# Reordered first products, a third gate bank, four column groups and eight products on a cleared region

## The chip, the cores and the metric

The kernel runs on one core of one Trainium2 chip. The time is the device time of one execution in microseconds (us), from the first to the last instruction and a little around them. The kernel before was timed in three runs; the traces come from one further execution, taken by the hardware profiler.

## The reference, cut to what matters

64 query tokens of 512 features attend to 6272 context rows of 512 features, and two more stages follow on the same 64 tokens. All of it is 32-bit.

```python
q  = layernorm(x) @ Wq + bq                 # 64 tokens, 32 heads of 128
k, v = split(ctx @ Wkv + bkv)               # 6272 keys, 8 key/value heads of 128
x  = x + softmax(q k^T / sqrt(128)) v @ Wo + bo      # 4 query heads share one key head
# quantised 4-bit weights W = NF4[codes] * scales, each with a rank-16 term (A, B)
z  = layernorm(x)
a  = (lin(z, Wq') + lin(z, Wk') + lin(z, Wv')) / 3
x1 = z + lin(a, Wo')
h  = silu(lin(x1, Wg)) * lin(x1, Wu)        # 1792 wide
x  = x + x1 + lin(h, Wd)                    # Wd: 1792 -> 512, low rank: (h A_down^T) B_down^T
x  = x + base and Fourier products of layernorm(x)
```

## The kernel before, in words

**The long loop.** The keys lie in 7 chunks of 896 (`CHUNK`), and each chunk is worked through for 8 key/value heads: 56 blocks. In a block TensorE (queue `pe`) makes the keys of the next head (`project_keys`), the scores of this head (`scores`), for every second head the values (`values`), it turns the probabilities (`turn_probs`) and multiplies those of the head before by the values (`prev_values`). Each 32-bit operand is split into a high part, rounded by ScalarE (queue `act`), and a low part, which VectorE (queue `dve`) makes by subtraction; a product is then three products (`split_matmuls`, L73 to L75). Beside that GpSimd (`pool`), ScalarE and VectorE expand one tile of the quantised weights per block: GpSimd narrows the codes (`narrow`) and makes four of eight straight lines (`line`), ScalarE four (`lines`), VectorE takes their maxima (`merge`), GpSimd joins and scales them (`join`), and the SyncE queue (`sp`) stores the tile in DRAM (`tile_out`). 56 tiles go out so; the last two, `NB` and `NB+1`, are kept in SBUF as `extra`.

**The order.** Each engine runs one list of instructions in the order written, held by semaphores. There is no planner: where a step stands in the list of its queue sets when it can run.

**The start.** `sp` loads x, the identity `ident` (both count on the semaphore `x_in`), chunks of the context, the query weights head by head (`load_wq`) and the key/value weights in eight pieces (`load_wkv`); `act` loads piece 0 and two parts of the context. VectorE normalises x once both x and `ident` are there (L1465), TensorE turns it (L875), VectorE copies it (L1477). Then the first keys are made: ScalarE rounds piece 0 and the four parts of the first context chunk (`round_wkv`, `round_first`), VectorE makes the low parts (`split_wkv`, `split_first`), and TensorE does 24 products, six for each part k (L880 to L882). After them come the query of head 0 (`query_product`, `query_turn`), then on ScalarE the keys' high parts (`round_keys`), the query's copy (`query_out`) and piece 1, on VectorE the keys' low parts (`split_keys`), the query's bias and split (`finish_query`) and piece 1. Only then the first block begins with its scores. GpSimd clears the first half of `acc`, the running output, right at the start (L576, semaphore `cleared`).

**The end.** After the last block TensorE projects the attention out and works through the quantised stage with weight tiles from a ring of 22 slots of two tiles each, which `sp` fills in order (`load_slot`); the loads from slot 35 on stand behind `scales_of(NB + 1)`, which waits until GpSimd has scaled tile `NB`. The gate and up products are made in three pairs of 256 columns each and a last half (`gated_pair`, `gated_last`), in two PSUM banks in turn (`GU_BANKS`); ScalarE takes the exponent, VectorE makes silu times up (L1552 to L1570, `h_ready`), TensorE turns the result (`turn_gated`, `h_turned`), VectorE copies it (`gated_t`, `h_t`), and six slots of the down weights follow (slots 40 to 45), then 14 small products for the low rank (`low_down`), the two tiles of `extra` and the low-rank product with `lb_d`. `late` are the loads of `lb_d` and the bias `bb_sb`.

Of the kernel before, what the change touches and what calls it, by code (L numbers as in the profile page):

```python
# [8 lines left out]
ACT = mybir.ActivationFunctionType  # L9
# [8 lines left out]
P = 128  # L18
HID = 512
KT = HID // P  # L20
# [108 lines left out]
def whole(nc, ctx_t, x, wq, bq, wkv, bk, bv, codes, scales, weights, wo, bo, lora_a, lora_a_down, lora_b, lora_b_down,  # L129
# [4 lines left out]
    with ExitStack() as st:  # L134
# [104 lines left out]
        def place_in_turn(place, tensors):  # L239
            got, skip = [], 0  # L240
            for name, shape in tensors:
# [17 lines left out]
        gate, ht = place_in_turn("pt_hi", (("gate", [P, 2, 5, 2 * P]), ("ht", [P, FT, TOK])))  # L259
        bb_sb, lb_d, w_four, z2t = place_in_turn("probs", (  # L260
            ("bb_sb", row), ("lb_d", [RANK, HID]), ("w_four", row), ("z2t", turned_rows)))
        e_small, = place_in_turn("o_t", (("e_small", [RANK, 4, TOK]),))
# [5 lines left out]
        WO_BANK, TURN_BANK, RANK_BANK, QKV_BANK, DOWN_BANK = 2, 3, 4, 5, 7  # L268
        GU_BANKS = (5, 6)

        w_in = [sem(f"w_in{i}") for i in range(WB)]
        w_used, small_in, late_in = sem("w_used"), sem("small_in"), sem("late_in")
        rows_in, gated_in = sem("rows_in"), sem("gated_in")
        x_in, vecs_in, coef_in = sem("x_in"), sem("vecs_in"), sem("coef_in")
        ln_step, var_ready, std_ready, xhat_ready = sem("ln_step0"), sem("var_ready0"), sem("std_ready0"), sem("xhat_ready0")
# [19 lines left out]
                  (lad[:], lora_a_down), (en[:], enc)]  # L295
        late = [(lb_d[:], lora_b_down)]
        late += [(bb_sb[HALVES[i], :], b_base[HALF_COLS[i]].partition_broadcast(TOK)) for i in range(2)]
# [56 lines left out]
        def _(sp):  # L354
# [57 lines left out]
            sp.dma_start(x_in_sb[:], x).then_inc(x_in, 16)  # L412
            sp.dma_start(ident[:], ident_in).then_inc(x_in, 16)
            for k in (1, 3):
# [75 lines left out]
            for slot in range(WB + 6, SLOTS):  # L490
                load_slot(slot)
                if slot == WB + 12:
                    scales_of(NB + 1)
            for dst, src in late:
                sp.dma_start(dst, src).then_inc(late_in, 16)
# [8 lines left out]
        def _(pool):  # L504
# [30 lines left out]
            def last_line(n):  # L535
                wait_apart(pool, merged, 6 * n + 1, pool_passed)
                line(7, 1)
# [87 lines left out]
            chunk(NCH - 2, 1, False)  # L625
            chunk(NCH - 1, 0, True)
            last_line(NB)
            narrow(NB + 1)
# [6 lines left out]
        def _(pe):  # L635
# [175 lines left out]
            def block_work(s, h, half, first, last):  # L811
# [58 lines left out]
                if i == 1:  # L870
                    query_turn(7)

            pe.wait_ge(xhat_ready, 1)
            for k in range(KT):
                t = nc.tensor.transpose(p_ot[:, k * TOK:(k + 1) * TOK], xhat[:, k * P:(k + 1) * P], ident[0:TOK, 0:TOK])  # L875
            t.then_inc(xt_psum, 1)
            pe.wait_ge(xt_ready, 1)
            pe.wait_ge(wkv_split, 1)
            for k in range(KT):
                pe.wait_ge(first_split, k + 1)  # L880
                for c in range(2):
                    project_keys(k_bank(NKV - 1, c), 0, 0, c, k)  # L882
            query_product(0)
            query_turn(0)
            for h in range(NKV):
# [76 lines left out]
            def gated_pair(c):  # L962

                bank = pb[GU_BANKS[c % 2]]
                if c == 0:
                    pe.wait_ge(gated_in, 16 * len(gateds))
                if c >= 2:
                    pe.wait_ge(step("h_ready"), c - 1)
                for k in range(KT):
                    stream_apart(bank, yts[k], k == 0)  # L970
                pe.wait_ge(step("e_gu"), 1)
                for j in range(2):
                    for i in range(2):
                        col = (2 * c + i) * 2 * P
                        m = nc.tensor.matmul(bank[HALVES[i], j * 2 * P:(j + 1) * 2 * P], e_small[:, 1 + j],
                                             lb_gu[:, j, col:col + 2 * P], start=False, stop=(j == 1))
                m.then_inc(step("gu_psum"), 1)

            def gated_last():

                bank = pb[GU_BANKS[GU_PAIRS % 2]]
                pe.wait_ge(step("h_ready"), GU_PAIRS - 1)
                for k in range(KT):
# [15 lines left out]
            def low_down(first, last):  # L999

                for t in range(first, last):
                    m = nc.tensor.matmul(pb[RANK_BANK][0:RANK, 0:TOK], lad[:, t], ht[:, t], start=(t == 0),
                                         stop=(t == FT - 1))
                return m

            for c in range(GU_PAIRS):
                gated_pair(c)
                if c >= 1:
                    turn_gated(c - 1)
            gated_last()  # L1010
            turn_gated(GU_PAIRS - 1)
            for n in range((FT - EXTRA) // 2):
                pe.wait_ge(step("h_t"), n // 2 + 1)
                stream(down_psum, [ht[:, 2 * n + j] for j in range(2)], n == 0)
                if n == 2:
                    turn_gated(GU_PAIRS)
# [9 lines left out]
            pe.wait_ge(step("e_d"), 1)  # L1026
            add_low_rank(down_psum, e_small[:, 3], lb_d[:]).then_inc(step("d_psum"), 1)
            mean_and_turn(1, xb)
# [20 lines left out]
        def _(act):  # L1049
# [134 lines left out]
            for k in range(KT):  # L1184
                round_first(k)
            nc.scalar.activation(alpha[:, 3, 0:1], ident[:, 0:1], ACT.Exp)
            act.wait_ge(vecs_in, 48)
            for c in range(2):
                round_keys(c, k_bank(NKV - 1, c), 0, c)
            query_out(0)  # L1190
            round_wkv(1)
            act.wait_ge(offsets_ready, 1)
            lines(0, True)
# [16 lines left out]
            act.wait_ge(w_used, WO_SLOTS + len(FOUR))  # L1210
            nc.scalar.activation(w_four[:], pb[DOWN_BANK][:, 0:TW // 2], ACT.Copy, scale=0.5).then_inc(step("folded_out"), 1)
            lines(NB + 1)
            load_table(ACT.Exp, 1)
            for c in range(GU_STEPS):
                w = 2 * P if c < GU_PAIRS else P
                act.wait_ge(step("gu_psum"), c + 1)
                if c >= 2:
                    act.wait_ge(step("one_plus"), c - 1)
                nc.scalar.activation(gate[:, c % 2, 0, 0:w], pb[GU_BANKS[c % 2]][:, 0:w], ACT.Exp,
                                     scale=-1.0).then_inc(step("exp_gate"), 1)  # L1220
# [6 lines left out]
        def _(dve):  # L1227
# [236 lines left out]

            dve.wait_ge(x_in, 32)  # L1465
            nc.vector.bn_stats(stats0[:], x_in_sb[:]).then_inc(ln_step, 1)
# [12 lines left out]
            for k in range(KT):  # L1479
                split_first(k)  # L1480
            dve.wait_ge(vecs_in, 48)
            for c in range(2):
                split_keys(c, k_bank(NKV - 1, c), 0, c)
            finish_query(0)
            split_wkv(1)
            dve.wait_ge(cleared, 1)
# [66 lines left out]
            for c in range(GU_STEPS):  # L1553

                bank = pb[GU_BANKS[c % 2]]
                w = 2 * P if c < GU_PAIRS else P
# [19 lines left out]
            dve.wait_ge(step("low_d"), 1)  # L1576
            nc.vector.tensor_copy(e_small[:, 3], pb[RANK_BANK][0:RANK, 0:TOK]).then_inc(step("e_d"), 1)
            dve.wait_ge(step("y_plus_xa"), 1)
# [98 lines left out]
```

## Time and profile before

| what | us |
|---|---|
| median of 3 runs | 1048.53 |
| lowest, highest run | 1047.41, 1054.11 |
| the profiled execution, its own time | 1053.61 |
| its span, first to last instruction | 1051.7 |
| TensorE busy in the span | 1017.2 (97%) |
| VectorE, ScalarE, GpSimd busy | 756.2, 589.9, 474.4 |

The span lies 1.9 us below the profiled execution's own time, and that execution is 5.1 us above the median. A saving is read off the span, in the stretches where TensorE waits or works at the lower clock; the 97% is a mean over a long middle part that is nearly full and two ends that are not.

### The profile page before, as it was taken

The numbers are of one execution on the slowest core, as the hardware profiler recorded it, in microseconds if no ns is written. First come the engines' busy times: TensorE is split into PE (matmuls) and PEld (weight loads), VectorE is DVE, ScalarE is ACT, GpSimd is POOL, SyncE is SP. The second block draws the span as 40 slices with busy tenths as digits, with TensorE's granted clock in tenths as the row PEclk, the third lists the DMA queues.
The fourth block names the chain that finished last, engine by engine and source line by source line (L and its number), as shares of the span: only waits on it lengthen the run. The fifth ranks groups of instructions, "written<-read, shape, count | busy, mean of one in ns | idle before, by whom it ended". The sixth has DMA issues, their size and how long they took to land.

```text
span 1051.7 us, 19647 instructions
## 1 busy us (share of the span) xinstructions
PE 1017.2 (97%) x7067; PEld 934.9 (89%) x7067; DVE 756.2 (72%) x1676; ACT 589.9 (56%) x1249; POOL 474.4 (45%) x636
## 2 busy tenths in 40 slices
PE   5989999999999999999999999999999999999988
PEld 4879889989999999999999999999999999999644
DVE  4566777768777787668777687777876778766664
ACT  4355565546655666556755566555665556655420
POOL 2334544454535554444544545445544445444330
PEclk9999999999999999999999999999999999999999
DMA  7851121222212122122211222211212215344966
GB/s 255 259 161 45 59 64 41 69 71 67 64 46 64 62 75 61 44 73 59 68 59 56 70 63 64 63 55 57 74 59 66 60 41 175 109 151 121 299 216 196
DMA packets 73440, 98.80 MB, mean 94 GB/s; under 512 B 8640, under 2 KB 42448, under 8 KB 73344
## 3 DMA queue, kind: packets, MB, share of 16 engines
q1 hardware_dynamic: 72352, 96.02, 29.6%
q10 hardware_dynamic: 896, 1.51, 0.4%
q8 instruction: 56, 0.92, 0.3%
q14 instruction: 40, 0.33, 0.1%
q0 software_dynamic: 96, 0.02, 0.0%
HBM read 82.71 MB, written 14.81 MB: 93 GB/s over the span
## 4 chain that ended last, share of the span: by engine, by line
PE 85%; DVE 5%; DMA 4%; POOL 2%; ACT 2%; issue 1%; POOLq 0%; SPq 0%; DVEq 0%
PE p_kv L73 18%; PE p_kv L74 18%; PE p_kv L75 18%; PE p_t L667 7%; PE p_o L73 4%; PE p_o L74 4%; PE p_o L75 4%; PE p_s L73 2%; PE p_s L74 2%; PE p_s L75 2%; PE p_s L750 2%; DMA expanded_weights<-slots 1%; DMA ctx_st<-in_ctx_t 1%; DVE slots L1279 1%; PE p_o L677 1%; PE p_ot L655 1%
## 5 line engine op out<-in xcount | busy, mean ns | idle before, releaser
L522 POOL TENSOR_SCALAR slots<-code 128x512 f32<-128x512 bf16 x232 | 154.6, 666 | 229.1 <-DVE slots L1283 158.3
L1279 DVE TENSOR_TENSOR slots<-slots 128x512 f32<-128x512 f32 x232 | 175.9, 758 | 3.0 <-POOL slots L522 1.2
L542 POOL TENSOR_TENSOR slots<-slots 128x512 f32<-128x512 f32 x58 | 75.8, 1306 | 205.7 <-DVE slots L1279 205.7
L1088 ACT ACTIVATE slots<-code,drop_and_offsets 128x512 f32<-128x512 bf16 x232 | 148.4, 714 | 30.7 <-POOL slots L542 30.7
L1232 DVE TENSOR_TENSOR v_lo<-p_kv,v_hi 128x256 fp32r<-128x256 f32 x196 | 83.2, 424 | 109.4 <-ACT v_hi L1053 108.5
L1234 DVE SCALAR_TENSOR_TENSOR k_lo<-p_kv,bk_sb,k_hi 128x448 fp32r<-128x448 f32 x112 | 76.3, 682 | 106.1 <-ACT k_hi L1053 105.2
L1244 DVE TENSOR_TENSOR pt_lo<-p_t,pt_hi 128x512 fp32r<-128x512 f32 x224 | 133.3, 617 | 25.6 <-ACT pt_hi L1064 25.6
L1053 ACT ACTIVATE v_hi<-p_kv 128x256 fp32r<-128x256 f32 x196 | 75.0, 384 | 136.5 <-PE p_kv L75 135.7
L1053 ACT ACTIVATE k_hi<-p_kv,bk_sb 128x448 fp32r<-128x448 f32 x112 | 70.9, 634 | 134.6 <-PE p_kv L75 133.9
L1064 ACT ACTIVATE pt_hi<-p_t 128x512 fp32r<-128x512 f32 x224 | 115.0, 542 | 41.7 <-PE p_t L667 41.7
L73 PE MATMUL p_kv<-wkv_hi,ctx_even_hi 128*128 128x256 f32 x448 | 126.4, 282 | 1.9 <-DVE v_lo L1232 1.9
L75 PE MATMUL p_kv<-wkv_hi,ctx_even_lo 128*128 128x256 f32 x448 | 125.9, 281 | 0.0
L74 PE MATMUL p_kv<-wkv_lo,ctx_even_hi 128*128 128x256 f32 x448 | 125.8, 281 | 0.0
L667 PE MATMUL p_t<-ident,probs 128*128 128x128 f32 x784 | 113.9, 273 | 4.0 <-DVE pt_lo L1244 3.1
L1131 ACT ACTIVATE probs<-probs,mins 128x896 f32<-128x896 f32 x112 | 115.5, 1032 | 0.0
L667 PEld LDWEIGHTS p_t<-ident,probs 128*128 128x128 f32 x784 | 95.0, 140 | 20.7 <-DVE pt_lo L1244 5.2
L73 PE MATMUL p_o<-pt_hi,v_hi 128*128 128x256 f32 x392 | 111.0, 283 | 0.0
L74 PE MATMUL p_o<-pt_lo,v_hi 128*128 128x256 f32 x392 | 110.9, 283 | 0.0
L75 PE MATMUL p_o<-pt_hi,v_lo 128*128 128x256 f32 x392 | 110.8, 283 | 0.0
L73 PE MATMUL p_kv<-ctx_even_hi,wkv_hi 128*128 128x448 f32 x256 | 100.2, 391 | 3.2 <-DVE ctx_even_lo L1393 2.7
L73 PE MATMUL p_kv<-wkv_hi,ctx_odd_hi 128*128 128x256 f32 x336 | 94.3, 281 | 1.5 <-DVE v_lo L1232 1.5
L74 PE MATMUL p_kv<-wkv_lo,ctx_odd_hi 128*128 128x256 f32 x336 | 95.1, 283 | 0.0
(224 smaller groups left out, 2692.5 us busy)
## 6 DMA issues: line engine op xcount, KB each, us to landing
code<-in_codes SPq DMA_DIRECT2D x58, 256.0 KB, 2.7
scale<-in_scales SPq DMA_DIRECT2D x116, 128.0 KB, 3.1
expanded_weights<-slots SPq DMA_DIRECT2D x56, 256.0 KB, 2.1
ctx_st<-in_ctx_t SPq DMA_DIRECT2D x96, 112.0 KB, 2.0
ring_hi<-expanded_weights SPq DMA_DIRECT2D x22, 256.0 KB, 5.4
ring_lo<-expanded_weights SPq DMA_DIRECT2D x22, 256.0 KB, 5.4
wq_hi<-in_wq SPq DMA_DIRECT2D x4, 1024.0 KB, 6.8
wq_lo<-in_wq SPq DMA_DIRECT2D x4, 1024.0 KB, 8.4
```

The costliest lines, as they stand in the source:

```text
L73: nc.tensor.matmul(out, hi, rhi, start=start, stop=False)
L74: nc.tensor.matmul(out, hi, rlo, start=False, stop=False)
L75: return nc.tensor.matmul(out, lo, rhi, start=False, stop=stop)
L522: nc.gpsimd.tensor_scalar(slots[:, slot, :], code16[:], LINES[j][0], LINES[j][1], ALU.mult, ALU.add).then_inc(pool_lines, 1)
L667: m = nc.tensor.transpose(p_t[:, c % 2, col:col + P], probs[:, r, t * P:(t + 1) * P], ident[:])
L1053: nc.scalar.activation(dst, src, ACT.Identity, bias=0.0 if bias is None else bias).then_inc(kv_rounded, 1)
L1064: nc.scalar.activation(pt_hi[:, 2 * c:2 * c + n, :].rearrange("p t q -> p (t q)"), p_t[:, c % 2, 0:n * ROWS], ACT.Copy).then_inc(pt_rounde ...
L1088: nc.scalar.activation(slots[:, slot, :], code16[:], ACT.Identity, bias=offsets[:, k:k + 1], scale=LINES[j][0]).then_inc(act_lines, 1)
L1131: nc.scalar.activation(probs[:, r, :], probs[:, r, :], ACT.Exp, bias=mins[:, h, r, now:now + 1], scale=-1.0, accum_out=rowsum[:, par, r:r ...
L1232: nc.vector.tensor_tensor(dst, src, hi.bitcast(F32), ALU.subtract).then_inc(kv_split, 1)
L1244: nc.vector.tensor_tensor(pt_lo[:, 2 * c:2 * c + n, :].rearrange("p t q -> p (t q)"), p_t[:, c % 2, 0:n * ROWS], pt_hi[:, 2 * c:2 * c + n, ...
L1279: nc.vector.tensor_tensor(slots[:, slot, :], slots[:, slot, :], slots[:, other, :], ALU.max).then_inc(merged, 1)
```

## The change

On TensorE, at the very start, five 32-bit products of the cleared part of `acc` with itself (128 rows, 256 columns, into a bank that nothing uses yet) stand ahead of the turn of x, and three more stand behind it. VectorE waits for x alone; the identity has a semaphore of its own, on which TensorE waits. The query product of head 0 moves in between the first products (behind k = 1) and its turn ahead of those of k = 3. On ScalarE piece 1 and the query's copy move ahead of the keys' high parts, on VectorE piece 1 and the query's split ahead of the keys' low parts. In the end the gate products get a third bank (2), so that the wait of the third pair for `h_ready` goes and the last half waits for the first result instead of the second; the turns of the gated rows move behind later products. The 14 small products of the low rank go to four groups of columns, the sum over the groups is made by `lb_d`, which is loaded four times into a region of 112 rows that GpSimd clears before; `sp` waits for that. ScalarE loads the table of the exponent ahead of the lines of tile `NB+1`.

```diff
-        bb_sb, lb_d, w_four, z2t = place_in_turn("probs", (
-            ("bb_sb", row), ("lb_d", [RANK, HID]), ("w_four", row), ("z2t", turned_rows)))
+        bb_sb, lb_d, e_d, w_four, z2t = place_in_turn("probs", (
+            ("bb_sb", row), ("lb_d", [3 * 32 + RANK, HID]), ("e_d", [3 * 32 + RANK, TOK]), ("w_four", row), ("z2t", turned_rows)))
-        GU_BANKS = (5, 6)
+        GU_BANKS = (5, 6, 2)
-        late = [(lb_d[:], lora_b_down)]
+        late = [(lb_d[32 * i:32 * i + RANK, :], lora_b_down) for i in range(4)]
@@ sync
-            sp.dma_start(ident[:], ident_in).then_inc(x_in, 16)
+            sp.dma_start(ident[:], ident_in).then_inc(ident_in_sb, 16)
...
+            sp.wait_ge(step("lb_d_cleared"), 1)
             for dst, src in late:
@@ gpsimd
             chunk(NCH - 1, 0, True)
+            wait_apart(pool, pt_psum, 4 * NB, pool_passed)
+            nc.gpsimd.memset(lb_d[:], 0.0).then_inc(step("lb_d_cleared"), 1)
             last_line(NB)
@@ tensor
+            pe.wait_ge(cleared, 1)
+            for _ in range(5):
+                nc.tensor.matmul(p_t[:, 0, 0:2 * P], acc[:, 0, 0, :], acc[:, 0, :, :].rearrange("p r d -> p (r d)"),
+                                 start=True, stop=True)
+            pe.wait_ge(ident_in_sb, 16)
             pe.wait_ge(xhat_ready, 1)
...
             pe.wait_ge(xt_ready, 1)
+            for _ in range(3):
+                nc.tensor.matmul(p_t[:, 0, 0:2 * P], acc[:, 0, 0, :], acc[:, 0, :, :].rearrange("p r d -> p (r d)"),
+                                 start=True, stop=True)
             pe.wait_ge(wkv_split, 1)
             for k in range(KT):
+                if k == KT - 1:
+                    query_turn(0)
                 pe.wait_ge(first_split, k + 1)
                 for c in range(2):
                     project_keys(k_bank(NKV - 1, c), 0, 0, c, k)
-            query_product(0)
-            query_turn(0)
+                if k == 1:
+                    query_product(0)
@@ gated_pair
-                bank = pb[GU_BANKS[c % 2]]
+                bank = pb[GU_BANKS[c % 3]]
-                if c >= 2:
-                    pe.wait_ge(step("h_ready"), c - 1)
@@ gated_last
-                bank = pb[GU_BANKS[GU_PAIRS % 2]]
-                pe.wait_ge(step("h_ready"), GU_PAIRS - 1)
+                bank = pb[GU_BANKS[GU_PAIRS % 3]]
+                pe.wait_ge(step("h_ready"), GU_PAIRS - 2)
@@ low_down
-                    m = nc.tensor.matmul(pb[RANK_BANK][0:RANK, 0:TOK], lad[:, t], ht[:, t], start=(t == 0),
-                                         stop=(t == FT - 1))
+                    group = t % 4 * 32
+                    m = nc.tensor.matmul(pb[RANK_BANK][group:group + RANK, 0:TOK], lad[:, t], ht[:, t], start=(t < 4),
+                                         stop=(t >= FT - 4))
...
             for c in range(GU_PAIRS):
                 gated_pair(c)
-                if c >= 1:
-                    turn_gated(c - 1)
+            turn_gated(0)
             gated_last()
-            turn_gated(GU_PAIRS - 1)
+            turn_gated(1)
             for n in range((FT - EXTRA) // 2):
                 pe.wait_ge(step("h_t"), n // 2 + 1)
                 stream(down_psum, [ht[:, 2 * n + j] for j in range(2)], n == 0)
-                if n == 2:
+                if n == 1:
+                    turn_gated(2)
+                if n == 3:
                     turn_gated(GU_PAIRS)
...
-            add_low_rank(down_psum, e_small[:, 3], lb_d[:]).then_inc(step("d_psum"), 1)
+            add_low_rank(down_psum, e_d[:], lb_d[:]).then_inc(step("d_psum"), 1)
@@ scalar
-            nc.scalar.activation(alpha[:, 3, 0:1], ident[:, 0:1], ACT.Exp)
+            act.wait_ge(offsets_ready, 1)
+            nc.scalar.activation(alpha[:, 3, 0:1], offsets[:, 0:1], ACT.Exp)
+            round_wkv(1)
+            query_out(0)
             act.wait_ge(vecs_in, 48)
             for c in range(2):
                 round_keys(c, k_bank(NKV - 1, c), 0, c)
-            query_out(0)
-            round_wkv(1)
-            act.wait_ge(offsets_ready, 1)
...
+            load_table(ACT.Exp, 1)
             lines(NB + 1)
-            load_table(ACT.Exp, 1)
@@ vector
-            dve.wait_ge(x_in, 32)
+            dve.wait_ge(x_in, 16)
...
+            split_wkv(1)
             dve.wait_ge(vecs_in, 48)
+            finish_query(0)
             for c in range(2):
                 split_keys(c, k_bank(NKV - 1, c), 0, c)
-            finish_query(0)
-            split_wkv(1)
...
-            nc.vector.tensor_copy(e_small[:, 3], pb[RANK_BANK][0:RANK, 0:TOK]).then_inc(step("e_d"), 1)
+            nc.vector.tensor_copy(e_d[:], pb[RANK_BANK][0:3 * 32 + RANK, 0:TOK]).then_inc(step("e_d"), 1)
```

## Rows read from the trace of the kernel before

**Rows 1.** PE's waits, by their sum: us in total, times, longest.

```profile
PE p_kv L73 <- DVE v_lo L1232: 3.4, 3, 1.5
...
PE p_o L677 <- DMA wq_lo<-in_wq: 2.3, 1, 2.3
```

**Rows 2.** Windows: stretch, length; busy us of PE, PEld, DVE, ACT, POOL; clock, DMA share, GB/s.

```profile
19.40:22.00 2.60, 2.12 (x19) 1.23 (x18) 1.28 (x2) 1.35 (x4) 1.71 (x3) 1.00 0.01 2
...
23.60:27.60 4.00, 3.97 (x12) 3.46 (x12) 2.95 (x7) 1.56 (x3) 0.00 (x0) 0.57 1.00 327
```

**Rows 3.** Chain of waits, start of the span: start us, us, what.

```profile
12.58 0.37 PE p_kv L74
...
18.02 0.21 PE p_kv L75
...
19.46 1.90 PE p_o L677 x16
...
22.29 0.50 DVE q_f L1381 x2
```

**Rows 4.** Timeline of the start: start us, us, engine, line, what.

```profile
1.00 0.95 POOL L576 MEMSET acc<- 128x1024 f32 x1
...
2.94 0.74 SPq L406 DMA_DIRECT2D wq_hi<-in_wq  x1
...
3.73 0.86 SPq L410 DMA_DIRECT2D wkv_raw<-in_wkv  x1
...
6.32 0.69 DVE L1466 BATCH_NORM_STATS2 stats<-x_in_sb 64x6 f32<-64x512 f32 x1 [6.32 <-DMA ident<-in_ident]
...
8.44 0.68 PE L875 MATMUL p_ot<-ident,xhat 64*128 64x64 f32 x4 [8.44 <-DVE xhat L1474]
...
10.64 4.09 DVE L1393 TENSOR_TENSOR ctx_even_lo<-ctx_raw,ctx_even_hi 128x896 fp32r<-128x896 f32 x4
...
19.70 1.28 DVE L1234 SCALAR_TENSOR_TENSOR k_lo<-p_kv,bk_sb,k_hi 128x448 fp32r<-128x448 f32 x2 [4.97 <-ACT k_hi L1053]
...
21.66 1.05 ACT L1120 ACTIVATE wkv_hi<-wkv_raw 128x1024 fp32r<-128x1024 f32 x1
...
23.49 1.22 DVE L1398 TENSOR_TENSOR wkv_lo<-wkv_raw,wkv_hi 128x1024 fp32r<-128x1024 f32 x1
...
23.63 0.47 PE L73 MATMUL p_s<-k_hi,q_hi 128*128 128x448 f32 x1 [1.37 <-DVE q_lo L1389]
```

**Rows 5.** DMA issues of the first 5 us: size, median us from issue to landing.

```profile
wq_hi<-in_wq SPq DMA_DIRECT2D x1, 1024.0 KB, 10.5
...
wkv_raw<-in_wkv SPq DMA_DIRECT2D x1, 512.0 KB, 11.2
x_in_sb<-in_x SPq DMA_DIRECT2D x1, 128.0 KB, 3.5
```

**Rows 6.** Timeline of the end.

```profile
1005.23 0.89 POOL L522 TENSOR_SCALAR slots<-code 128x512 f32<-128x512 bf16 x1 [4.85 <-DVE slots L1283]
...
1020.86 1.08 PE L975 MATMUL p_o<-lb_gu,e_small 16*64 16x256 f32 x8
...
1023.82 0.44 PE L958 MATMUL p_kv<-ident,gate 128*128 128x128 f32 x2 [1.88 <-DVE gate L1568]
```

**Rows 7.** Loads of down slots 44 and 45: issues, then us to landing.

```profile
L385 SPq DMA_DIRECT2D ring_odd<-expanded_weights x4: 376/432/543, 1029.2 to 1030.7; - x4
...
DMA to landing us min/median/max: 5.7/6.2/7.1
```

**Rows 8.** Windows of the end, columns as in rows 2.

```profile
1010.00:1012.00 2.00, 1.07 (x8) 0.38 (x6) 0.71 (x2) 0.00 (x0) 0.00 (x0) 1.00 0.00 2
...
1024.00:1026.00 2.00, 2.00 (x8) 0.60 (x9) 1.93 (x4) 0.00 (x0) 0.72 (x1) 0.55 1.00 331
```

**Rows 9.** Chain of waits, end of the span.

```profile
1040.22 1.67 PE p_t L1002 x28
...
1045.33 0.65 PE p_t L1033 x16
```

More of the change, by code:

```diff
@@ L273, in whole @@
         rows_in, gated_in = sem("rows_in"), sem("gated_in")
-        x_in, vecs_in, coef_in = sem("x_in"), sem("vecs_in"), sem("coef_in")
+        x_in, ident_in_sb, vecs_in, coef_in = sem("x_in"), sem("ident_in_sb"), sem("vecs_in"), sem("coef_in")
         ln_step, var_ready, std_ready, xhat_ready = sem("ln_step0"), sem("var_ready0"), sem("std_ready0"), sem("xhat_ready0")
@@ L1218, in _ @@
                     act.wait_ge(step("one_plus"), c - 1)
-                nc.scalar.activation(gate[:, c % 2, 0, 0:w], pb[GU_BANKS[c % 2]][:, 0:w], ACT.Exp,
+                nc.scalar.activation(gate[:, c % 2, 0, 0:w], pb[GU_BANKS[c % 3]][:, 0:w], ACT.Exp,
                                      scale=-1.0).then_inc(step("exp_gate"), 1)
@@ L1553, in _ @@
             for c in range(GU_STEPS):
-                bank = pb[GU_BANKS[c % 2]]
+                bank = pb[GU_BANKS[c % 3]]
                 w = 2 * P if c < GU_PAIRS else P
```

## The prediction

> **What bounds the kernel now.** I read the page first: TensorE is busy 97% of the span, and the 40 slices show that only the first and the last two fall short. Then I asked for its waits by sum: beyond the first wait for x no entry is over 3.4 us, and over the long loop they come to three of 0.9 to 1.5 us [rows 1]. So the middle can't be bought with waits, and this change does not touch it. What is left is the two ends. For these I read windows, the chain and the timeline side by side, looking at two things: what holds TensorE back, and how far apart its products start.
>
> At the start, the chain steps by 0.37 us from one 448-column product to the next at 12.58, and by 0.21 at 18.02 [rows 3]. That is 1.2 against 2.4 GHz. From 23.6 to 27.6 the granted clock is 0.57, that is mostly the lower level again [rows 2]; TensorE had stood still for part of the time before. The first block's scores begin at 23.63, released by the query's low part [rows 4]. And between 19.4 and 22.0 the DMA engines do nothing (share 0.01) [rows 2], because the next query weights wait for the first query product, which ends at 21.4 [rows 3].
>
> At the end, TensorE waits 1.88 us for the first gated result at 1023.82 [rows 6], and the clock then falls to 0.55 [rows 8]. But the loads of the last down slots are issued from 1029.2 to 1030.7 and land up to 7.1 us later, at 1037.8 [rows 7], while the down products end at 1040.22 [rows 9]. The load queue had been empty from 1010 on (share 0.00) [rows 8], held by the wait for tile NB's scaling; the change leaves that wait where it is.
>
> **The start, step by step.** x lands 3.5 us after its issue at 0.75 [rows 5], so at 4.25; VectorE began at 6.32, held by the identity [rows 4]. The norm moves 2 us ahead, and the turn of x from 8.44 to about 6.4; it needs the identity too, which is there at 6.3. No gain by itself.
>
> The five products can begin when the clear of `acc` ends at 1.95 [rows 4]. The trace has no 32-bit product of 128 by 256. Nearest is the query product: eight in two halves that run together, four full-width rounds in 1.90 us [rows 3], 0.475 each at the higher clock and at most 0.95 at the lower. Five take 4.3 to 4.75 us, until 6.3 to 6.7, and so cost the turn 0 to 0.3 us. The three behind it end by 10.5 at the latest. None of it is on the path, as follows.
>
> VectorE splits the four context parts from 10.64 to 14.73 [rows 4]. With an earlier start they are bound by the context's landing, and end between 13.2 and 14.7. TensorE does k = 0 and 1 by 12.6 (higher clock, 12 steps of 0.205 = 2.5 us behind the first split at 10.2) to 14.0. The query product needs weights issued at 2.94 that land 10.5 later, at 13.4 [rows 4, 5]: 13.4 to 15.3, at worst 15.9. Piece 1 is issued at 3.73 and lands 11.2 later, at 14.9 [rows 4, 5], and this is now the head of the chain, since ScalarE and VectorE have it ahead of the query: ScalarE 1.05 to 16.0, VectorE 1.22 to 17.2 [rows 4]; then the query's bias and split, 22.29 to 23.58 [rows 3, 4], 1.3 us to 18.5; then the first keys' low part, half of 1.28 [rows 4], to 19.2. TensorE meanwhile turns the query at 16.5 and does k = 3 by 18.2, which ScalarE rounds in time. Scores begin at 19.3 instead of 23.63: **4.3 us**. If they run at the higher clock, as TensorE has then been at work almost without a stop since 13.4, the 12 products take 12 x 0.205 = 2.5 instead of 4.2 us: **1.8 us** more. Sum 6.1.
>
> What follows is fed by DMAs issued on the queries' progress. The transfers were idle for the 2.6 us of that window [rows 2], and with the partly filled stretches on both sides about 4.0; with the query product at 15.3 that hole closes, and they can move ahead by as much, and a little more where the share is below 1 later. The last query weights already make TensorE wait 2.3 us [rows 1]. So between 4.0 (the transfers bind) and 6.1 (TensorE binds) I take **5.2**, the middle, as both kinds of waits appear there.
>
> **The end, step by step.** Third bank: the third pair runs on from 1021.9, where the second ends [rows 6], not from 1024.2. The idle 1.88 us and the stretch at the lower clock (3.4 us at half rate, 1.7 us lost) [rows 6, 8] would give 3.6 us. But the slots it needs land one by one behind the issues that resume after 1015.8: I follow them, and from slot 37 on TensorE is at the load's heels. The last slot lands at 1037.8 at the latest [rows 7], its products take 0.9, so down ends at 1038.7: **1.5 us** of 3.6. If the landings are not all at the maximum it is up to 2.4, if they are delayed 0. The turns that stand later delay nothing, as VectorE takes them up only after its next reciprocal and products, and its copies come before the down slots that read them land.
>
> Low rank: 28 records take 1.67 us [rows 9]. In four column groups, the nearest row is 16 records in two groups in 0.65 [rows 9]. Lower bound of time 0.65, upper the 1.67 (groups that don't overlap). I take 0.7, as that row is the same 64-column product: **1.0 us**. The product of 112 rows with `lb_d` costs what the one of 16 did, by columns. GpSimd's clear is 512 columns, half of 0.95 [rows 4]: 0.5 us, in the 4.85 us that GpSimd stood before 1005.23 [rows 6]. Behind it stand tile NB's lines, which wait for VectorE anyway. Were that idle gone, it would cost 0.5 us on the scaling of NB, and so on all loads behind. Its wait for the last turned probabilities is over 12 us before. `sp` issues three more loads of 0.43 each ahead of bias and last weights: 1.3 us, on loads that are used only after the down slots and the low rank, so nothing; with that cover gone, at most the 1.3 us. The exponent's table ahead of the lines: the first gate exponent comes 1 us sooner, but VectorE works on merges until 1020.8, so nothing.
>
> **Sum.** 5.2 + 1.5 + 1.0 = 7.7 us. Against the profiled execution, 1053.6 - 7.7 = 1045.9; against the median of the runs, which is 5.1 lower, 1048.5 - 7.7 = 1040.8. I say **1041**. 1% is 10.5 us, about what a measurement of this kernel can tell from no change.
>
> **A rule on the clock.** The trace shows that TensorE got to the higher level between 12.58 and 18.02 [rows 3], some 5.4 us after the first keys began, and fell back near 24 and 1024 after stretches with waits [rows 2, 8]. The Trainium skill, "TensorE: Matmul & The Clock Gate", Part 1, says that the point of rise shifts from run to run because the monitor is not tied to the kernel's start, and Part 4 that products in transpose mode don't count as work for it. By this rule five products, a turn of x, a wait and three products need not lift the clock at all; that is rival A. No run here shows it yet.
>
> **Rivals.**
> A, the eight products don't keep the clock up. The first real products then run at 0.37 until 5.4 us after 10.2, that is 15.6: k = 0 and 1 end at 14.7, the query product at 17.0, k = 3 at 19.9, scores at 20.7, still at the higher clock. That is 1.4 us less, a gain of 6.3 in all: 1042. For it: the two idle stretches around them. Against: 4.3 us of work without a gap. Chance 0.15.
>
> B, the transfers swallow the start. Piece 1 or the later query weights come no sooner relative to the block that uses them, the 2.3 us wait grows by what was won. Gain 2 at the start, 1.5 to 2.5 at the end: about 1044.5. For it: share 1.00 at 327 GB/s [rows 2]. Chance 0.20.
>
> C, it doesn't do what it says: the start's lead is lost again in the first two chunks, where ScalarE's and VectorE's lists bind in turns, and the down slots land late. Then nothing, 1046 to 1050. Chance 0.10.
>
> D, more: the lower clock at 23.6 and the 2.3 us wait both vanish and the end is held by the median landing: 6.1 + 2.3 + 2.4 + 1.0 = 11.8, so 1036.7. Chance 0.12.
>
> E, slower: the long loop settles into another phase, in which TensorE waits for VectorE's `v_lo` once per chunk, 1.5 us each as the longest of the three it has [rows 1]. Seven chunks are 10.5 us, less 7.7: 2.8 slower, 1051.3. It decides from the sixth added wait on. For it: such waits exist at irregular places. Against: nothing in the loop is changed, and they are three in 56 blocks. Chance 0.05.
>
> **How the numbers follow.** The forecast itself has 0.38; A lies by its side, so 0.53 lies in 1039 to 1043.5. The range reaches over B and the near half of C and D: 1036.5 to 1047, leaving out 0.06 below and 0.10 above. Faster by over 1% (below 1038.0) is D and a small part of the forecast's low side, 0.14; slower by over 1% only an extreme of E, 0.03; within 1% the rest, 0.83.
>
> **What would show it.** In the trace of the changed kernel: first scores at 19.3 (not 23.6), the products of 448 columns 0.21 apart from the first, no window with a clock near 0.57 around 20 to 27, and DMA share near 1 from 16 on. The wait for the query weights near 70 tells between 4.0 and 6.1. In the end: no wait before the third pair, down products that wait for loads (not for VectorE), `low_down` near 0.7. I am wrong if piece 1's landing moves, if first scores start past 21, or if TensorE's waits between 130 and 960 exceed 5 us in sum.

## The result, and the profile after

The changed kernel takes 1042.19 us (median of 10 runs, 1040.59 to 1044.89) against 1049.91 us before (10 runs in the same comparison). The ratio is 0.9927, with a 95% interval from 0.9912 to 0.9943: 7.7 us less, 0.7%. That interval is 3.3 us wide, so a measurement of this kernel tells smaller changes than the 1% that the prediction gave it. The profiled execution has a span of 1042.2 us, 9.5 us below the 1051.7 of the one before. Two single executions differ by more than the medians do; how that comes is taken up below.

The windows of the start in the kernel after, with the columns and the first two stretches of [rows 2]:

```profile
19.40:22.00 2.60, 1.89 (x10) 1.80 (x11) 2.06 (x5) 1.92 (x4) 1.82 (x3) 1.00 1.03 372
23.60:27.60 4.00, 4.00 (x35) 3.47 (x32) 1.08 (x4) 2.81 (x7) 0.00 (x0) 1.00 0.84 226
```

In the first the DMA share is 1.03 where it was 0.01: the hole between the first loads and the second batch is closed. In the second TensorE has 35 instructions at a clock of 1.00, where it had 12 at 0.57. One caution on the column of the clock. In the kernel before it reads 1.00 at the start too, while the first products there are 0.37 us apart:

```profile
11.90:17.40 5.50, 5.50 (x15) 4.88 (x16) 2.83 (x3) 1.70 (x3) 0.00 (x0) 1.00 1.04 356
```

In these traces the column does not show the lower level ahead of its first fall. There the level is read from the step: 0.37 us is also the step of these products where the column reads 0.50 (from 24.6 on in the kernel before).

The timeline of the start, kernel after:

```profile
2.01 4.63 PE L878 MATMUL p_t<-acc 128*128 128x256 f32 x10 [2.01 <-POOL acc L577]
...
3.69 0.69 DVE L1479 BATCH_NORM_STATS2 stats<-x_in_sb 64x6 f32<-64x512 f32 x1 [3.69 <-DMA x_in_sb<-in_x]
...
7.56 1.56 PE L887 MATMUL p_t<-acc 128*128 128x256 f32 x6 [0.52 <-DVE xt L1490]
...
11.36 0.44 PE L73 MATMUL p_kv<-ctx_even_hi,wkv_hi 128*128 128x448 f32 x1 [2.24 <-DVE ctx_even_lo L1406]
...
11.84 0.36 PE L75 MATMUL p_kv<-ctx_even_hi,wkv_lo 128*128 128x448 f32 x1
12.04 0.36 PE L73 MATMUL p_kv<-ctx_even_hi,wkv_hi 128*128 128x448 f32 x1
...
14.32 1.95 PE L680 MATMUL p_o<-wq_hi,xt 128*64 128x256 f32 x16 [0.32 <-DMA wq_hi<-in_wq]
...
20.11 0.44 PE L73 MATMUL p_s<-k_hi,q_hi 128*128 128x448 f32 x1 [0.99 <-DVE k_lo L1247]
...
24.56 0.38 PE L73 MATMUL p_kv<-wkv_hi,ctx_even_hi 128*128 128x256 f32 x1
```

x is taken up at 3.69 instead of 6.32, the five products end at 6.6, the three at 9.1 (each of the eight has two records). The first keys start at 11.36, hardly before the 11.87 of before, but they follow each other at 0.20 us from the second on, not at 0.37. Scores begin at 20.11 instead of 23.63, and the first values, the last row, at 24.56 instead of the 29.70 of the kernel before:

```profile
29.70 0.38 PE L73 MATMUL p_kv<-wkv_hi,ctx_even_hi 128*128 128x256 f32 x1
```

The chain of waits of the same kernel shows who sets the start of the scores:

```profile
3.60 12.17 DMA wkv_raw<-in_wkv
15.78 0.02 issue
15.80 1.07 ACT wkv_hi L1133
16.86 0.02 issue
16.89 1.06 DVE wkv_lo L1411
...
18.03 0.49 DVE q_f L1394 x2
...
18.88 0.42 DVE q_lo L1402
19.30 0.67 DVE k_lo L1247
```

It is the chain that the prediction wrote down, with the landing of piece 1 12.2 us behind its issue instead of 11.2.

The end, first in the chain of waits (as in [rows 9]), then PE's waits for the loads, then PE's waits for gated results in the kernel before:

```profile
1022.76 7.93 DMA ring_odd<-expanded_weights
1030.69 0.14 issue
1030.83 1.08 PE p_ot L753 x8
1031.91 0.56 PE p_t L1014 x28
```

```profile
PE p_ot L753 <- DMA ring_odd<-expanded_weights: 1.6, 1, 1.6
...
PE p_s L761 <- DMA ring_lo<-expanded_weights: 0.9, 1, 0.9
...
PE p_ot L753 <- DMA ring_lo<-expanded_weights: 0.4, 1, 0.4
```

```profile
PE p_kv L958 <- DVE gate L1568: 2.6, 2, 1.9
```

No wait for a gated result is left, but three for ring slots, 2.9 us together, have come. The low rank's 28 records take 0.56 instead of 1.67 us. As a measure of the end I take the time from the row that starts xa, the stream behind the attention, to the row that starts xb, the stream behind the down products: 1000.89 to 1043.60 before, 42.7 us; 992.69 to 1034.03 after, 41.3 us.

```profile
992.69 0.42 DVE L1353 SCALAR_TENSOR_TENSOR xa<-p_s,x_bo 128x256 f32<-128x256 f32 x1 [1.00 <-PE p_s L753]
...
1034.03 0.42 DVE L1353 SCALAR_TENSOR_TENSOR xb<-p_ot,y_xa 128x256 f32<-128x256 f32 x1 [1.29 <-PE p_ot L804]
```

So of the 9.5 us between the two profiles 1.4 lie in the end. From 29.70 to 24.56 the first values moved by 5.1 us, and the remaining 3 us were won in between.

### The profile page after: what moved, and what is told of

Same layout as the page of the kernel before. It is cut to its first block, busy times and chain, and to the rows that moved or that the text cites. A ratio compares the mean times of both kernels' runs of the same rounds, so it can differ in the third digit from the quotient of the medians.

```text
span 1042.2 us, 19683 instructions
## 1 busy us (share of the span) xinstructions
PE 1016.8 (98%) x7083; PEld 933.9 (90%) x7083; DVE 758.4 (73%) x1676; ACT 590.3 (57%) x1249; POOL 474.3 (46%) x637
## 4 chain that ended last, share of the span: by engine, by line
PE 86%; DMA 5%; DVE 4%; ACT 2%; POOL 2%; SPq 1%; issue 1%; POOLq 0%; DVEq 0%
PE p_kv L73 18%; PE p_kv L74 18%; PE p_kv L75 18%; PE p_t L670 7%; PE p_o L73 4%; PE p_o L74 4%; PE p_o L75 4%; PE p_s L73 2%; PE p_s L74 2%; PE p_s L75 2%; PE p_s L753 2%; DMA wkv_raw<-in_wkv 1%; PE p_o L680 1%; PE p_ot L658 1%; DMA expanded_weights<-slots 1%; DMA ctx_st<-in_ctx_t 1%
## 5 line engine op out<-in xcount | busy, mean ns | idle before, releaser
L1077 ACT ACTIVATE pt_hi<-p_t 128x512 fp32r<-128x512 f32 x224 | 115.0, 542 | 41.6 <-PE p_t L670 41.5
L1144 ACT ACTIVATE probs<-probs,mins 128x896 f32<-128x896 f32 x112 | 115.5, 1032 | 0.0
```

Source lines behind the costliest of these rows:

```text
L1077: nc.scalar.activation(pt_hi[:, 2 * c:2 * c + n, :].rearrange("p t q -> p (t q)"), p_t[:, c % 2, 0:n * ROWS], ACT.Copy).then_inc(pt_rounde ...
L1144: nc.scalar.activation(probs[:, r, :], probs[:, r, :], ACT.Exp, bias=mins[:, h, r, now:now + 1], scale=-1.0, accum_out=rowsum[:, par, r:r ...
```

## The experiments

The median of an experiment rests on 6 to 12 runs, and its interval is 2.6 to 4.7 us wide. The kernel after itself, measured a second time (`after_again`), came out at 1043.04 instead of 1042.19, so a difference of about 1 us between two experiments says nothing. `two_banks`, `scales_two_banks`, `five_only` and `piece_later` ran on another chip than the other experiments; the ratio to the kernel before, measured beside each, is the fairer number for them. Single profiles spread as well. The end of the kernel after stands unchanged in six profiles, and xa to xb takes 40.7 (`piece_later`), 40.9 (`end_only`), 41.3, 41.3 (`five_only`), 41.5 (`no_eight`) and 43.9 us (`after_again`).

**The two ends apart.** `start_only` is the kernel after with the end of before; `end_only` the one with the start of before.

```diff
 start_only, against the kernel after
-        GU_BANKS = (5, 6, 2)
+        GU_BANKS = (5, 6)
...
-                    group = t % 4 * 32
...
 end_only, against the kernel after
-            for _ in range(5):
...
-            for _ in range(3):
...
-            dve.wait_ge(x_in, 16)
+            dve.wait_ge(x_in, 32)
...
-                if k == 1:
-                    query_product(0)
+            query_product(0)
+            query_turn(0)
```

> The kernel after with its end as it was before (two gate banks, turns in the old places, one column group, lb_d loaded once, table behind the lines); the start is the changed one. Theory (the start gives most): the changed kernel's values of block 0 begin at 24.6 instead of 29.7 and the end's saving in its trace is only 1.4 us (1.0 of it the low rank), so this one gains 5 to 7.5 us of the 7.7 on the kernel before: 1042 to 1045 against 1050. Rival (the end gives as much as the 2.5 us I forecast and more): gain of at most 5 us, 1045 or above.

> The kernel after with its start as it was before (no eight products, x and identity on one semaphore, old order on TensorE, ScalarE and VectorE); the end is the changed one. Theory: gain of 1 to 2 us, of which low_down 1.0 (1.67 to 0.63) and the down slots 0.2 to 0.5, since their loads hold them. Rival (third bank gives its 3.6 us where the loads land in time): gain of 3.5 to 4.6 us. If the two ends add up, start_only and this one together give the 7.7 us.

Measured: 1043.64 and 1047.69 us against 1049.50 (ratios 0.9942 [0.9922, 0.9963] and 0.9980 [0.9963, 0.9997]), gains of 5.9 and 1.8 us, with intervals from 3.9 to 8.2 and from 0.3 to 3.9. The medians add up to the 7.7 of the whole, closer than the intervals warrant. The start gives about three quarters. In `end_only` xa to xb takes 40.9 us with four waits for ring slots, 2.6 us together.

**The loads of the ring moved out of the way.** `scales_later` changes one line of the kernel after:

```diff
-                if slot == WB + 12:
+                if slot == SLOTS - 3:
                     scales_of(NB + 1)
```

> The kernel after with one line moved: the load of the last scales, at which the load queue waits some 11.5 us for tile NB, stands behind slot 43 instead of slot 34. So the ring slots 35 to 43 are loaded in those empty 11 us. Theory (the third bank's saving was swallowed by these loads): the waits of the down products for ring slots (1.6, 0.9, 0.4 us in the kernel after) go, TensorE is then bound by VectorE's gate steps; 2 to 3 us faster than the kernel after. Rival (the gate steps on VectorE set the pace anyway, or the scales come late for tile NB+1): less than 0.7 us, and the wait appears before the down products on ht, or before the extra tiles.

Measured: 1039.09 us, ratio to before 0.9903 [0.9880, 0.9925], 3.1 us faster than the kernel after by the medians. In its trace xa to xb takes 37.4 instead of 41.3 us and no wait for a ring slot is left; `more_behind`, which has the same end, takes 37.4 us too. The expectation named 2 to 3 us; the end alone gave 4. The windows of its end, and the row of its low rank:

```profile
1012.00:1016.00 4.00, 4.00 (x22) 1.35 (x22) 2.76 (x5) 0.38 (x1) 2.54 (x3) 1.00 1.09 348
1026.00:1031.00 5.00, 4.97 (x55) 2.69 (x55) 3.02 (x10) 0.00 (x0) 0.00 (x0) 1.00 0.13 49
```

```profile
1030.77 0.63 PE L1014 MATMUL p_t<-ht,lad 128*16 128x64 f32 x28
```

TensorE is busy in 4.00 of 4.00 and 4.97 of 5.00 us, and the loads are over (share 0.13) while the down products still run. In the kernel after they were the last to come.

**Is it the bank or the loads?** `two_banks` is the kernel after with two gate banks and the turns in their old places, `scales_two_banks` is `two_banks` with the line of `scales_later`.

```diff
 two_banks, against the kernel after
-        GU_BANKS = (5, 6, 2)
+        GU_BANKS = (5, 6)
...
+                if c >= 2:
+                    pe.wait_ge(step("h_ready"), c - 1)
...
-                pe.wait_ge(step("h_ready"), GU_PAIRS - 2)
+                pe.wait_ge(step("h_ready"), GU_PAIRS - 1)
```

> The kernel after with two gate banks and the turns of the gated rows in their old places; the four column groups and the early table stay. From the row that starts xa to the row that starts xb it took 42.7 us before and 41.3 in the kernel after. Theory (the loads of the last ring slots set the end, so the bank is worth almost nothing and the low rank's 1.0 us is nearly the whole): 41.5 to 42.0 us here, and at most 0.6 us slower than the kernel after (1042.2). Rival (the bank gives 1.5 us, as I forecast): 42.8 us or more, 1.5 us slower.

> The kernel two_banks with the load of the last scales behind slot 43, as in scales_later, which took 37.4 us from xa to xb. Theory (bank and loads hide each other: each alone gives little, both together 4 us): without the bank TensorE waits 1.9 us for the first gated result and the clock falls after it, so 40 to 41.5 us here, 2.5 to 4 us slower than scales_later (1039.1). Rival (the loads alone were the bound and the bank is idle): within 0.5 us of 37.4.

Measured: 1043.17 us (0.9940 [0.9921, 0.9960]) and 1043.60 us (0.9948 [0.9929, 0.9967]); xa to xb 41.6 us in both. So the third bank alone is worth nothing that these runs can tell (41.6 against 40.7 to 43.9 us with it), the moved loads alone nothing either, and both together 4.2 us, from 41.6 to 37.4. The medians agree: `scales_two_banks` lies 0.4 us from `two_banks` and 4.5 us above `scales_later`. Each hides the other. In `scales_two_banks` TensorE waits for VectorE and then works at the lower clock:

```profile
1013.83 0.69 PE L971 MATMUL p_kv<-ident,gate 128*128 128x128 f32 x2 [2.18 <-DVE gate L1582]
...
1014.45 1.98 PE L761 MATMUL p_t<-ring_hi,yt 128*64 128x512 f32 x4
```

The granted clock reads 0.50 from 1013.80 to 1016.50. The 1.98 us for four records are 1.08 at most where the clock is up.

**The eight products.** `no_eight` leaves them out of the kernel after, `five_only` leaves out the three behind the turn of x.

```diff
 no_eight leaves out both loops, five_only the second
             pe.wait_ge(cleared, 1)
-            for _ in range(5):
...
             pe.wait_ge(xt_ready, 1)
-            for _ in range(3):
```

> The kernel after without the eight products on the cleared region, all else kept. Theory (landings of the query weights and of piece 1 head the chain; the eight products only buy the clock): first products start at the same 11.4 but 0.37 apart until some 5 us later, so k = 0 and 1 end near 15.8 instead of 14.0, the query product near 18, first scores near 21.5 instead of 20.1, and the scores may fall to the lower clock: 1.4 to 3 us slower than the kernel after. Rival A (the eight did nothing, the clock would have risen anyway): within 0.5 us of the kernel after, and the step of the first products is 0.20 or the same in both.

> The kernel after without the three products behind the turn of x; the five ahead of it stay. no_eight was 3.1 us slower than the kernel after. Theory (the five raise the clock, the three keep it up until the first split at 10.1 to 11.4): the clock is lost again in most executions, first products 0.37 apart as in no_eight, 1.5 to 3 us slower than the kernel after. Rival (the rise once made lasts over the 4 us without work): within 0.5 us of the kernel after (1042.2).

Measured: 1045.32 us (0.9957 [0.9940, 0.9974]) and 1045.92 us (0.9964 [0.9950, 0.9978]), 3.1 and 3.7 us slower than the kernel after, 2.3 and 2.9 slower than its second measurement. The first steps of `no_eight`:

```profile
10.86 0.71 PE L73 MATMUL p_kv<-ctx_even_hi,wkv_hi 128*128 128x448 f32 x1 [4.29 <-DVE ctx_even_lo L1399]
11.37 0.57 PE L74 MATMUL p_kv<-ctx_even_lo,wkv_hi 128*128 128x448 f32 x1
11.74 0.57 PE L75 MATMUL p_kv<-ctx_even_hi,wkv_lo 128*128 128x448 f32 x1
12.12 0.57 PE L73 MATMUL p_kv<-ctx_even_hi,wkv_hi 128*128 128x448 f32 x1
...
21.80 0.44 PE L73 MATMUL p_s<-k_hi,q_hi 128*128 128x448 f32 x1 [1.23 <-DVE k_lo L1240]
```

Scores begin at 21.8, 1.7 us behind the kernel after. Piece 1 landed at 15.2 here, not at 15.8; against `two_banks`, where it landed at 15.2 too and scores begin at 19.52, the loss is 2.3 us. The query product, which in the kernel after waits for its weights at 14.3, starts at 15.6 here, straight behind the slow products. `five_only` looks the same from 11.1 on (the step is 0.37, scores at 21.6) although its five products were made and the clock had risen. The turn behind them takes 0.43 us, where it took 0.68 in the kernel before, and the granted clock falls to 0.50 near 8.7, in the 4.65 us without work before the first keys:

```profile
11.12 0.71 PE L73 MATMUL p_kv<-ctx_even_hi,wkv_hi 128*128 128x448 f32 x1 [4.65 <-DVE ctx_even_lo L1403]
11.62 0.57 PE L74 MATMUL p_kv<-ctx_even_lo,wkv_hi 128*128 128x448 f32 x1
```

A rise that is not kept up is lost. The five without the three are worth nothing that these runs can tell. Of the 5.9 us of the start the eight products thus hold 2.3 to 3.1; the rest is left to the new order of the steps, which was not run by itself.

**Does the clock stay up in every execution?** The profile of `scales_later` itself, whose start is that of the kernel after, has this:

```profile
11.30:12.60 1.30, 1.28 (x6) 1.19 (x7) 1.20 (x2) 1.30 (x2) 0.00 (x0) 0.91 1.03 397
12.60:15.20 2.60, 2.60 (x10) 1.86 (x8) 1.77 (x2) 1.97 (x3) 0.00 (x0) 0.50 1.04 358
```

The granted clock falls to 0.50, the lower level, in the middle of the first products, although TensorE is busy there; it had stood still for 2.7 us before. Scores begin at 21.45 and the values at 25.91, 1.35 us later than in the kernel after. That is rival A. In the other profiles with the three products the engine stood still for 0.6 to 2.2 us at that place and the products kept their 0.20; the one with the longest gap is the one in which the clock fell. How often it falls these runs don't tell. `more_behind` has eight products instead of three there, on top of `scales_later`, and `after_again` is the kernel after once more.

```diff
 more_behind, against scales_later
-            for _ in range(3):
+            for _ in range(8):
```

> The kernel scales_later (1039.1) with eight instead of three products behind the turn of x. In the profile of scales_later the clock fell at 12.5 all the same, and scores began at 21.5 instead of 20.1. Theory (work up to the first split keeps the clock up in every execution): five products more are 2.1 us, they end at 10.7 to 11.3, about when the first split comes; first products 0.20 apart, median 0.3 to 0.8 us below scales_later, and its highest run closer to its lowest. Rival (they run at the lower clock or past the first split and delay it): the same or up to 1.5 us slower.

> The kernel after once more, for a second profile of the same instructions and on the same chip as the two below. Theory (TensorE's waits for v_lo in the long loop come by chance, and so does the fall of the clock between the three products and the first split): median 1042 to 1043; number and sum of the v_lo waits differ from the first profile (two, 2.0 us); the landings of the first query weights and of piece 1 differ from 14.3 and 15.8 by up to 1 us. Rival (they are the kernel's own): the same two waits at the same places.

Measured: `more_behind` 1039.49 us (0.9914 [0.9897, 0.9931]), 1038.46 to 1040.23; `scales_later` had 1038.19 to 1042.89. The medians can't be told apart, so the 0.3 to 0.8 us is not shown. What its profile shows is a gap of 0.56 us instead of 2.69:

```profile
6.84 3.72 PE L887 MATMUL p_t<-acc 128*128 128x256 f32 x16 [0.52 <-DVE xt L1490]
...
11.12 0.44 PE L73 MATMUL p_kv<-ctx_even_hi,wkv_hi 128*128 128x448 f32 x1 [0.56 <-DVE ctx_even_lo L1406]
11.40 0.36 PE L74 MATMUL p_kv<-ctx_even_lo,wkv_hi 128*128 128x448 f32 x1
11.60 0.36 PE L75 MATMUL p_kv<-ctx_even_hi,wkv_lo 128*128 128x448 f32 x1
```

`after_again` gave 1043.04 us (0.9945 [0.9926, 0.9964]). Its profiled execution, the same instructions as the kernel after, differs in several places. The three products took 2.92 us instead of 1.56, so the rise came later than in the first profile; the first keys, at 0.20 us, have it. Piece 1 landed at 15.2 instead of 15.8, and in the end a wait of 1.8 us for a slot was followed by a low rank at about half speed (granted clock 0.50 from 1032 to 1034). That brings xa to xb to 43.9 us and the execution to 1046.01. TensorE's waits for `v_lo` are again two, of 1.9 us in all, so their number did not differ as expected; over the thirteen profiles of this study there are between none and three of them, with 0 to 3.4 us. The two rows that show the clock's effect:

```profile
7.78 2.92 PE L887 MATMUL p_t<-acc 128*128 128x256 f32 x6 [0.52 <-DVE xt L1490]
...
1032.94 1.04 PE L1014 MATMUL p_t<-ht,lad 128*16 128x64 f32 x28
```

**The order of piece 1.** `piece_later`:

```diff
-            round_wkv(1)
             query_out(0)
             act.wait_ge(vecs_in, 48)
             for c in range(2):
                 round_keys(c, k_bank(NKV - 1, c), 0, c)
+            round_wkv(1)
...
-            split_wkv(1)
             dve.wait_ge(vecs_in, 48)
             finish_query(0)
             for c in range(2):
                 split_keys(c, k_bank(NKV - 1, c), 0, c)
+            split_wkv(1)
```

> The kernel after with piece 1 behind the query and the keys on ScalarE and on VectorE (order there: query's copy, keys, piece 1; query's split, keys, piece 1). In the kernel after piece 1 lands at 15.8 and the query's split ends at 19.3, scores begin at 20.1. Theory (piece 1's landing and its 1.23 us on VectorE head the chain): query's copy at 16.3 instead of 16.8, split from 17.2 instead of 18.0, scores at 19.3 to 19.5, 0.5 to 0.9 us earlier. Rival (its wait is only moved: the values of block 0 then wait for piece 1's low part, and ScalarE's lines come later): values begin at 24.5 as before, no gain.

Measured: 1042.78 us (0.9940 [0.9919, 0.9960]): no gain. Scores begin at 19.48, as the theory had it, but `two_banks`, with piece 1 in the changed place and landed at 15.2, begins at 19.52. With the query's weights landing where they do, TensorE turns the query behind k = 2 in any case, at 16.9 in both. In the profiles with piece 1 in the changed place that kept the higher clock, scores begin 4.3 to 4.5 us behind the landing of piece 1 (14.8 and 19.09 up to 15.8 and 20.11). So its chain is the last to end there, but the query's own stands right behind it: 19.48 against 19.52. Moving piece 1 can give 0.6 us where it lands as late as in the profile after, and nothing where it lands at 15.2.

**The low rank.** `one_group`:

```diff
-                    group = t % 4 * 32
-                    m = nc.tensor.matmul(pb[RANK_BANK][group:group + RANK, 0:TOK], lad[:, t], ht[:, t], start=(t < 4),
-                                         stop=(t >= FT - 4))
+                    m = nc.tensor.matmul(pb[RANK_BANK][0:RANK, 0:TOK], lad[:, t], ht[:, t], start=(t == 0),
+                                         stop=(t == FT - 1))
```

> The kernel after with one column group for the low rank: lb_d of 16 rows loaded once, no clear on GpSimd, no wait on the load queue for it. Theory (low_down stands behind the last ring slot, on the path whatever the loads do): its 28 records take 1.67 to 1.74 instead of 0.63 us, 42.3 to 42.5 us from xa to xb instead of 41.3, 0.7 to 1.2 us slower than the kernel after. Rival (the three loads and the clear cost as much as the groups give): within 0.4 us.

Measured: 1044.23 us (0.9960 [0.9948, 0.9973]), 2.0 us slower than the kernel after and 1.2 slower than its second measurement, with this row:

```profile
1029.57 1.74 PE L1010 MATMUL p_t<-ht,lad 128*16 128x64 f32 x28
```

The 1.1 us are there. Xa to xb came out at 41.3 us all the same, since in this execution the slots cost 0.7 us of waiting instead of 2.9. The medians don't isolate the low rank either. `one_group` was slowed by a fall of the clock behind xb in its profile (last section), and `start_only`, which has one group and two banks as well, took 1043.64. The 1.1 us are shown by the row, which reads 1.74 us in all three kernels with one group and 0.63 in nine of the ten profiles with four.

## Why the prediction was right, and where its terms were off

The forecast was 7.7 us and 1041; measured are 7.7 us and 1042.2, from a median of before that came out 1.4 us above the one shown. The sum was right, its parts less so, and that both gains read 7.7 is in part luck. The interval of the gain is 6.0 to 9.2 us, and the second measurement of the same kernel gave 5.9. Two errors also cancelled: the third bank was put 0.5 to 1.4 us too high, the start 0.7 too low. And rival A's time, 1042, lies nearer to 1042.19 than my own; only the traces tell them apart.

**The start: 5.2 forecast, 5.9 measured** by `start_only`, with 5.2 inside its interval of 3.9 to 8.2. The chain was the predicted one, step by step: weights of the query, piece 1, ScalarE 1.05, VectorE 1.22, the query's split, the keys. Scores came 0.8 us later than the 19.3 written down, for piece 1 landed at 15.8 instead of 14.9, which I had named as a sign of being wrong; in other executions it lands at 14.8 to 15.6 and scores begin at 19.1 to 20.0. The lower clock in the scores was put at 1.8 us, though 4.2 less 2.5 is 1.7; from the scores to the first values it took 6.07 us before and 4.45 after, so it was worth 1.6. The cut from 6.1 to 5.2, for what the transfers would swallow, has its size by luck. The first values moved by 5.1 us (5.6 in `start_only`), short of 6.1 since piece 1 landed late. The wait for the last query weights took nothing more away: it is 1.4 us in the kernel after and 2.1 in `start_only`, against 2.3 before, and 1.1 to 2.8 in the other profiles with the new order of the start.

I had put the eight products down at no gain by themselves, and rival A, the clock not kept up, at 1.4 us. The rival's mechanism is real and showed itself unasked in one profile, where the values came 1.35 us late. But its price without any of the products is 2.3 to 3.1 us in the medians, not 1.4. In front of the scores 2.3 us are lost at an equal landing of piece 1; whether there is more, these runs don't tell. I had priced it from scores at 19.3 to scores at 20.7, and in the three profiles with the lower clock they begin at 21.5 to 21.8. Part 1 of "TensorE: Matmul & The Clock Gate" in the Trainium skill says that the point of the rise shifts from run to run; the two profiles of the same kernel agree, with the three products at 1.56 and at 2.92 us. Its Part 4, that transposes don't count as work, is neither shown nor refuted by these runs.

**Third bank: 1.5 forecast, 0.1 to 1.0 measured.** This term failed in size: `two_banks` is 1.0 us slower than the kernel after by the medians and 0.1 slower than its second measurement, and the traces differ by 0.3, less than those of one kernel do. The reasoning was right that the load sets the end. What it missed is that I took the landings of before as fixed. The issues did come at the same distance behind tile NB, 13.3 us from the last scales to slot 44, but the last tile of the slots landed 7.9 us behind its issue, not 7.1 [rows 7], and two waits for slots stand before it. Counted from the row of xa, the last landing came at 38.0 us instead of 36.9, and the down products ended at 39.2 instead of 39.3. The prediction names this case ("if they are delayed 0") and gives it no weight: it took the longest landing of before for the latest possible one. `scales_later` against `scales_two_banks` shows what the bank is worth when the landings don't bind: 4.2 us. The early table of the exponent was not run by itself.

**Low rank: 1.0 forecast, 1.1 in the traces.** The medians of `one_group` say 1.2 to 2.0, that of `start_only` allows less. Taking it from the row of 16 records in two groups was sound. The clear on GpSimd took 0.52 us at 992.1, in the idle time named for it, and the three further loads delayed nothing that TensorE waited for.

**The rest of the 9.5 us.** The profiles of before and after differ by 1.8 us more than the medians. In the long loop, where nothing was changed, TensorE's waits for `v_lo` were 3.4 us in the one and 2.0 in the other, and over all profiles they run from 0 to 3.4. So those 1.4 us are chance; the rest is not located. It also speaks against rival E: with the changed start they don't grow.

Rival B is refuted by `start_only` with its 5.9 us, rival C by the result. Rival D, 11.8 us, is nearly what `scales_later` reaches (10.4), though on another path: it needs the loads to be moved.

## What to carry to other kernels

When two things hold the same stretch, a wait for a result and a load that comes just in time, an edit to either shows nothing; look where the load queue stands still before it, and move that first. Here one line, which lets the queue fill the ring while it would wait for something else, turned a third bank that showed nothing into one worth 4.2 us, and gave the fastest kernel of this study. A clock that was raised with filler products has to be kept up to the first real product: a gap of 4.65 us lost it, one of 2.7 us did too, gaps up to 2.2 us did not, here. And a single profile of such a start is one draw from several.

## What the runs showed of the hardware

The granted clock fell while TensorE was fully busy: in `scales_later` it goes to 0.50 about 1 us after work had begun again (the stretch from 12.60 to 15.20 above); the engine had stood still for 2.7 us before that. In `one_group` the fall comes at the very end of the kernel, where the chain is made of short products and waits, and the time from xb to the end of the last product's row is 6.5 us, where it is 4.8 in the kernels before and after:

```profile
1033.00:1035.00 2.00, 0.91 (x10) 0.67 (x12) 1.51 (x5) 0.00 (x0) 0.00 (x0) 0.95 0.00 0
1035.00:1038.00 3.00, 3.00 (x32) 2.05 (x30) 1.09 (x6) 0.20 (x1) 0.00 (x0) 0.50 0.02 5
```

The 28 records of the low rank took 0.56 to 0.63 us in four column groups against 1.67 to 1.74 in one: a factor of 2.8 to 3, not 4.
